# Transfers into the stacks of four attention layers dealt anew over SyncE, ScalarE and GpSimd, in one fused kernel on one core

## The chip, the cores and the metric

One Trainium2 chip, one core. The metric is device time in microseconds of one execution, the median of several runs. Engines: TensorE (PE, with PEld for its weight loads), VectorE (DVE), ScalarE (ACT), GpSimd (POOL), SyncE (SP). Three of them issue DMA transfers here: SP, ACT and POOL; the rows mark these as SPq, ACTq and POOL or POOLq.

## The reference

A picture of 16 x 16 places with 192 channels, batch 1, goes through four residual layers, each with a group norm (32 groups) ahead. All have 12 heads of 16 dimensions and 256 places.

```
x = x + L0(gn(x))   # attention, scores + rel_h (by row) + rel_w (by column)
x = x + L1(gn(x))   # layer norm, attention with rotated q and k and a bias by "same row",
                    # residual, layer norm, feed-forward 192-768-192 with gelu, residual
x = x + L2(gn(x))   # 7x7 neighbourhood attention plus 16 register keys and values
x = x + L3(gn(x))   # like L0, with other weights

qr = q.reshape(B * nh, H, W, hd)                    # the bias of L0 and L3
rel_h = einsum('bhwc,hkc->bhwk', qr, Rh)
rel_w = einsum('bhwc,wkc->bhwk', qr, Rw)
attn = softmax(q * scale @ k.T + rel_h[..., :, None] + rel_w[..., None, :])
```

## The kernel before

Each engine has a program written out by hand, and semaphores order them; no scheduler moves anything. A layer runs so: statistics and norm, projection to queries, keys and values, then scores, exponents, values by head, output projection and residual.

The scores of a head are one matmul over a stack of 128 partitions. QS (queries, two buffers for even and odd layers) and KS (keys) hold for each head four rows for the maxima and the same-place bias and seven blocks of 16 rows (`rows_of(stack, block)` takes one): Q_HIGH, Q_LOW and Q_AGAIN are the high and low parts of queries against the high and low parts of keys (a float32 product made of three float32r ones); ROW_HIGH, COL_HIGH, ROW_LOW, COL_LOW are the terms of the relative bias (L0, L3), of the same-row bias (L1) or of the mask (L2). The parts are computed in tiles that lie by other partitions: QH, QL, KH, KL (96 partitions, two halves of six heads; index 0 and 1), QHL (queries of layers 0 and 3, three groups of four heads), ROWH, ROWL, COLH, COLL (bias terms, three groups). A DMA moves each into its rows of the stack, 96, 64 or 32 KB at a time. ACT makes the high parts, DVE the low ones, right after the projections.

Who waits for what: PE computes each head's scores twice. `for_maxima` (L1014) lays a head's scores by query, DVE takes the maximum (L845), `turn_maxima` (L1028) turns it and ACT copies it into the stack (L631); `scores` (L1050) then computes them by key, ACT takes exponents (L639) and `values` (L1075) multiplies. PE waits before head 0 for the semaphores "q stack", "k stack" and "first rows" (all the transfers of head group 0 or half 0); before head 6 for "later heads" and "later keys" (half 1); in layers 0 and 3 before head 4 for "second heads" and "second queries" and before head 8 for "third heads" and "third queries". The order on PE at a layer's start is: maxima of heads 0, 1, 2, warming matmuls (L936), maxima 3, turn 0, maxima 4, turn 1, scores 0, maxima 5, scores 1, maxima 6, turn 2, maxima 7, values of heads 0 and 1, scores 2, maxima 8. Maxima h may start when DVE has done h - 2 heads.

Who issues: SP's `move` (L336) waits for the signal of its source and issues, in program order, so whatever stands behind a waiting transfer waits too. In layers 1 and 2 it moves by half: QH twice, QL (half 0 of layer 2: POOL), KL. In layers 0 and 3 it moves the queries of group 0, the keys of half 0, then `row_terms` of group 0 and 1, KL of half 1, `row_terms` of group 2; in layer 0 then the later weights (L329). POOL moves the queries of groups 1 and 2 (L464, L467), ROWL of group 0 (L473) and all column terms (L450), in layers 1 and 2 the low rows of half 0's keys (L442), and, after layer 0's last scores, twelve small transfers of the register keys (L523) and four of the mask (L526), which layer 2 needs. Between these POOL computes: bias rows of layer 1 (L495), scaling of key weights (L426), in layer 1 the second half of QF and QL (L514, L516). ACT moves the high keys of half 0 of layers 1 and 2 and both high blocks of half 1 of all layers (L591).

## Time and profile before

| | |
|---|---|
| time, median of 3 runs (lowest to highest) | 154.02 us (153.69 to 154.68) |
| the profiled execution: time, span | 154.34 us, 152.4 us |
| PE busy | 138.8 us (91%) |
| DVE, ACT, POOL busy | 94.3, 68.4, 51.3 us (62, 45, 34%) |
| granted clock of PE | 1.0 over the whole span |
| transfers | 13.55 MB, mean 89 GB/s |

The span is what the profile covers; the time has about 1.9 us more around it. All starts in the rows are counted from the span's start. Layer 0's attention heads begin near 17 us, those of layer 1 near 54, of layer 2 near 98, of layer 3 near 131. Busy shares say little here, since PE is kept busy by warming matmuls too; what counts is where PE waits.

### The profile page before, as it was taken

The page shows a single profiled execution, that of the slowest core. Times are in us where ns is not written, and L with a number is a line of the kernel's source. Part 1 is how long each engine was busy: PE and PEld are TensorE (multiplying, and loading weights), DVE is VectorE, ACT ScalarE, POOL GpSimd, SP SyncE. Part 2 cuts the span into 40 slices and gives each one's busy share as a digit, 9 for nine tenths or more (in the row PEclk, how much of TensorE's full clock was granted, in tenths as well). Part 3 has the DMA queues.
Part 4 walks back from the last instruction along what each step waited for, and adds up shares of the span by engine and source line. Part 5 has one row for each costly group of instructions (what it writes and reads, how often), then busy time and mean ns, then how long its engine had stood idle before and what let it go on. Part 6 is the DMA issues. An engine that isn't in the chain of part 4 may idle for free.

```text
span 152.4 us, 2651 instructions
## 1 busy us (share of the span) xinstructions
PE 138.8 (91%) x914; PEld 93.3 (61%) x914; DVE 94.3 (62%) x246; ACT 68.4 (45%) x158; POOL 51.3 (34%) x92
## 2 busy tenths in 40 slices
PE   6789979999989898999899999689999999979992
PEld 2468656545667575655478747567655679656551
DVE  6885678556749997775630074494546665767462
ACT  4665156842222236770155344055752364166820
POOL 7788988730300499900000002600000077300000
PEclk9999999999999999999999999999999999999999
DMA  5728638999300573900000001900000036810001
GB/s 156 198 54 220 163 97 269 275 275 324 83 0 0 155 163 17 205 0 0 4 0 0 0 0 34 264 13 4 0 0 4 0 114 184 189 33 2 0 0 52
DMA packets 12573, 13.55 MB, mean 89 GB/s; under 512 B 4145, under 2 KB 10433, under 8 KB 12561
## 3 DMA queue, kind: packets, MB, share of 16 engines
q1 hardware_dynamic: 7664, 9.34, 21.5%
q0 software_dynamic: 3424, 2.91, 9.4%
q10 hardware_dynamic: 1472, 1.14, 2.7%
q8 instruction: 7, 0.11, 0.3%
q14 instruction: 6, 0.04, 0.1%
HBM read 6.82 MB, written 0.20 MB: 46 GB/s over the span
## 4 chain that ended last, share of the span: by engine, by line
PE 61%; DVE 13%; DMA 11%; ACT 7%; issue 3%; SPq 3%; POOL 0%; DVEq 0%; ACTq 0%
PE PC L1075 14%; PE RING L1050 8%; DMA KS<-KL 7%; PE RING L936 4%; PE PA L1085 4%; PE RING L1276 4%; PE RING L1014 3%; DVE NM L845 3%; DMA HOT<-in_hot 3%; SPq L336 3%; PE PB L1085 3%; PE PB L1014 2%; PE PA L1282 2%; PE PB L1282 2%; PE PC L971 2%
## 5 line engine op out<-in xcount | busy, mean ns | idle before, releaser
L639 ACT ACTIVATE PR<-RING 128x512 f32<-128x512 f32 (+1 forms) x48 | 25.7, 553 | 9.4 <-PE RING L1050 9.1
L1075 PE MATMUL PC<-PR,VX 128*32 128x256 f32 (+1 forms) x192 | 23.6, 369 | 0.0
L936 PE MATMUL RING<-WARM 128*128 128x512 bf16 x78 | 22.3, 400 | 1.3 <-POOL WARM L395 1.3
L845 DVE TENSOR_REDUCE NM<-RING 128x2 fp32r<-128x512 f32 (+1 forms) x32 | 20.2, 653 | 5.1 <-PE RING L1014 5.1
L1050 PE MATMUL RING<-QS,KS 128*128 128x256 f32 (+1 forms) x96 | 20.2, 305 | 0.4 <-ACT QS L631 0.2
L1050 PEld LDWEIGHTS RING<-QS,KS 128*128 128x128 f32 x96 | 13.9, 189 | 7.8 <-issue 5.1
L631 ACT ACTIVATE QS<-PA 4x512 fp32r<-4x512 f32 (+1 forms) x20 | 10.6, 532 | 15.3 <-PE PA L1028 15.3
L1014 PE MATMUL RING<-KS,QS 128*128 128x256 f32 (+1 forms) x64 | 13.2, 297 | 0.9 <-DVE NM L845 0.8
L1075 PEld LDWEIGHTS PC<-PR,VX 128*32 128x32 f32 x192 | 8.6, 109 | 8.2 <-ACT PR L639 1.3
L852 DVE STREAM_TRANSPOSE TURNED_U<-PC 128x256 f32<-128x256 f32 x12 | 5.4, 450 | 12.8 <-PE PC L1075 12.8
L845 DVE TENSOR_REDUCE NM<-PB 128x2 fp32r<-128x512 f32 (+1 forms) x16 | 10.5, 656 | 4.3 <-PE PB L1014 4.2
L464 POOL DMA_DIRECT2D QS<-QHL x8 | 4.1, 516 | 25.0 <-ACT QHL L614 25.0
L936 PEld LDWEIGHTS RING<-WARM 128*128 128x128 bf16 x78 | 7.5, 107 | 7.1 <-issue 1.4
L1014 PE MATMUL PB<-KS,QS 128*128 128x256 f32 (+1 forms) x32 | 7.4, 312 | 4.2 <-DMA KS<-KL 3.7
L1014 PEld LDWEIGHTS RING<-KS,QS 128*128 128x128 f32 x64 | 9.4, 189 | 3.0 <-DVE NM L845 2.6
L439 POOL DMA_DIRECT2D QS<-QL x1 | 0.5, 538 | 29.8 <-DVE QL L795 29.8
L1014 PEld LDWEIGHTS PB<-KS,QS 128*128 128x128 f32 x32 | 5.0, 188 | 7.5 <-DVE NM L845 2.7
L563 ACT ACTIVATE SQUARED<-X 96x256 f32<-96x256 f32 x8 | 3.3, 415 | 11.4 <-DVE X L909 7.9
L426 POOL TENSOR_SCALAR WQKV<-WQKV 96x384 f32<-96x384 f32 x4 | 5.4, 1362 | 8.8 <-DMA WQKV<-in_w 8.6
L1085 PE MATMUL PA<-O,WO 128*96 128x256 f32 x24 | 7.8, 405 | 0.0
L1085 PE MATMUL PB<-O,WO 128*96 128x256 f32 x24 | 7.1, 379 | 0.0
L495 POOL TENSOR_SCALAR QS<-HOT,ABS 128x256 fp32r<-128x256 f32 x12 | 6.7, 554 | 1.2
(186 smaller groups left out, 270.6 us busy)
## 6 DMA issues: line engine op xcount, KB each, us to landing
WQKV<-in_w SPq DMA_DIRECT2D x2, 576.0 KB, 8.4
WO<-in_wo SPq DMA_DIRECT2D x4, 288.0 KB, 8.9
W<-in_ff SPq DMA_DIRECT2D x2, 576.0 KB, 9.6
KS<-KH ACTq DMA_DIRECT2D x10, 96.0 KB, 3.0
WQKV<-in_w SPq DMA_DIRECT2D x2, 432.0 KB, 4.9
QS<-QHL POOLq DMA_DIRECT2D x12, 64.0 KB, 2.7
KS<-KL SPq DMA_DIRECT2D x8, 96.0 KB, 3.1
QS<-QH SPq DMA_DIRECT2D x8, 96.0 KB, 2.5
```

Of the source, the lines that this page charges most:

```text
L426: g.tensor_scalar(w[:, :, first:first + C], w[:, :, first:first + C], QK_SCALE, None, ALU.mult)\
L495: g.tensor_scalar(QS[1][:, h, :], HOT[:, :], ABS[:, 2, h:h + 1], ABS[:, 1, h:h + 1], ALU.mult, ALU.add).then_inc(sem("ab rows"), 1)
L631: A(QS[l % 2][0:GH, heads[0]:heads[-1] + 1, :], turn_bank(t)[0:GH, None, 0:T].to_broadcast([GH, len(heads), T]), ACT.Copy).then_inc(sem("m ...
L639: A(PR[:, h % NPR, 0:n], exponents(l, h)[:, 0:n], ACT.Exp).then_inc(sem("probs"), 1)
L845: V.tensor_reduce(NM[:, TURN_OF[h], :, h % GH], MAXIMA[h % 3][:, 0:2 * n_keys].rearrange("p (q k) -> p q k", q=2), AX.X, ALU.max, negate=T ...
L936: M(bank, WARM[:, 0:P], WARM[:, :], start=True, stop=True)
L1014: ins = M(s[:, q * n_keys:(q + 1) * n_keys], QS[l % 2][:, h, q * P:(q + 1) * P], KS[:, h, keys], start=True, stop=True)
L1050: ins = M(half(s, l, k), KS[:, h, KEY0 + k * P:KEY0 + (k + 1) * P], QS[l % 2][:, h, reach(l, k)], start=True, stop=True)
L1075: ins = M(columns(h)[:, reach(l, k)], VX[:, k, h, :], half(PR[:, h % NPR, :], l, k), start=(k == 0 and l != 2), stop=(k == 1), skip_group_ ...
L1085: ins = M(y_psum(m), WO[l][:, g, m * CC:(m + 1) * CC], in_order(O[g][:, :]) if l in REL_LAYERS else O[g][:, :], start=(g == 0), stop=(g == ...
L1276: ins = M(s[:, i * T:(i + 1) * T], W1[:, k, c * P:(c + 1) * P], XN[:, k, :], start=(k == 0), stop=(k == NC - 1))
L1282: ins = M(y_psum(m), W2[:, c, m * CC:(m + 1) * CC], hidden(c), start=(c == 0), stop=(c == FM - 1), skip_group_check=True)
```

## The change

The same transfers are made, but for others to issue, and in another order.

- Layers 0 and 3: COLL of group 0 goes from POOL to SP (after the first ROWH pair). ROWL of groups 1 and 2 goes from SP to POOL, behind that group's column terms. ROWH of group 2 goes from SP to ACT, behind the second half's keys. SP's later weights wait for "later heads" and the new "third rows".
- Layer 1: QL goes from SP to POOL, half 0 in place of the low keys, half 1 right after POOL has made it. The low keys of half 0 go from POOL to ACT. The register keys and the mask wait for the first four scores of layer 1 instead of the last of layer 0.
- Layer 2: on SP and on ACT, the moves of half 1 wait for "v psum", the end of the value matmuls (L989).

```diff
@@ SyncE, layers 1 and 2 @@
+                        if i and l == 2:
+                            sync.wait_ge(*upto("v psum", 2, 1))
                         for block in (Q_HIGH, Q_AGAIN):
                             move("qh", rows_of(queries, block)[:, heads], QH[:, i, :], "later heads" if i else "q stack", i + 1)
-                        if i or l == 1:
-                            move("ql", rows_of(queries, Q_LOW)[:, heads], QL[:, i, :], "later heads" if i else "q stack", i + 1)
+                        if i and l == 2:
+                            move("ql", rows_of(queries, Q_LOW)[:, heads], QL[:, i, :], "later heads", i + 1)
@@ SyncE, layers 0 and 3 @@
-                row_terms(0)
-                row_terms(1)
+                high_rows(0)
+                move_group("rel l", COL_LOW, COLL, 0, 4)
+                high_rows(1)
                 move("kl", rows_of(KS, Q_AGAIN, KEY0, REG1)[:, HPC:NH], KL[:, 1, :], "later heads", NC)
-                row_terms(2)
                 if l == 0:
 
-                    sync.wait_ge(*upto("third heads", 0, 4 * 16))
+                    sync.wait_ge(*upto("later heads", 0, 16))
+                    sync.wait_ge(*upto("third rows", 0, 2 * 16))
                     load(later_loads)
@@ GpSimd @@
+            def move_low_rows(l, g, done):
+
+                for r in range(2):
+                    places = slice(r * P, (r + 1) * P)
+                    first = 0 if r else GH
+                    pool.dma_start(rows_of(QS[l % 2], ROW_LOW)[:, g * GH:(g + 1) * GH, places].bitcast(F32),
+                                   ROWL[first:first + 64, g, places].bitcast(F32)).then_inc(sem(done), 16)
...
-                for name, block, src in (("rel h", COL_HIGH, COLH), ("rel l", COL_LOW, COLL)):
+                for name, block, src in (("rel h", COL_HIGH, COLH), ("rel l", COL_LOW, COLL))[:2 if g else 1]:
...
                     for group, done in enumerate(("first rows", "second queries", "third queries")):
+                        if group == 0:
+                            move_low_rows(l, 0, done)
                         move_column_terms(l, group, done)
+                        if group:
+                            move_low_rows(l, group, done)
...
-                    pool.wait_ge(*upto("scores", 0, NH))
+                    pool.wait_ge(*upto("ql", 1, 2))
+                    pool.dma_start(rows_of(QS[1], Q_LOW)[:, HPC:NH].bitcast(F32), QL[:, 1, :].bitcast(F32))\
+                        .then_inc(sem("later queries"), 16)
+
+                    pool.wait_ge(*upto("scores", 1, GH))
@@ ScalarE @@
                 act.wait_ge(*upto("kh", l, i + 1))
+                if i and l == 2:
+                    act.wait_ge(*upto("v psum", 2, 1))
                 heads = slice(i * HPC, (i + 1) * HPC)
-                for block in (Q_HIGH, Q_LOW) if i else (Q_HIGH,):
+                for block in (Q_HIGH, Q_LOW) if i or l == 1 else (Q_HIGH,):
...
                     move_keys(l, 1)
+                    for r in range(2):
+                        places = slice(r * P, (r + 1) * P)
+                        first = 0 if r else GH
+                        act.dma_start(rows_of(QS[l % 2], ROW_HIGH)[:, 2 * GH:NH, places].bitcast(F32),
+                                      ROWH[first:first + 64, 2, places].bitcast(F32)).then_inc(sem("third rows"), 16)
@@ TensorE, before maxima h @@
                 if h == HPC:
+                    if l == 1:
+                        pe.wait_ge(sem("later queries"), 16)
                     pe.wait_ge(*upto("later heads", l, signals["later heads"][l]))
...
-                    pe.wait_ge(*upto(f"{which} heads", l, 4 * 16))
-                    pe.wait_ge(*upto(f"{which} queries", l, 5 * 16))
+                    pe.wait_ge(*upto("second heads" if h == GH else "third rows", l, 2 * 16))
+                    pe.wait_ge(*upto("second queries" if h == GH else "third queries", l, 7 * 16))
```

The order of issues, as it stands in the two programs. GpSimd in layer 0, from ROWL of group 0 to the first instruction that is not a transfer, before (layer 3 has the same):

```order
25 L473 DMA QS<-ROWL 16x4x128 [waits rel_l]
26 L473 DMA QS<-ROWL 16x4x128
27 L450 DMA QS<-COLH 16x4x256 [waits rel_h]
28 L450 DMA QS<-COLL 16x4x256 [waits rel_l]
29 L450 DMA QS<-COLH 16x4x256 [waits rel_h]
30 L450 DMA QS<-COLL 16x4x256 [waits rel_l]
31 L450 DMA QS<-COLH 16x4x256 [waits rel_h]
32 L450 DMA QS<-COLL 16x4x256 [waits rel_l]
33 L411 MEMSET VR 128x384
```

and in the changed kernel (L452 is ROWL, L460 the column terms):

```order
25 L452 DMA QS<-ROWL 16x4x128 [waits rel_l]
26 L452 DMA QS<-ROWL 16x4x128
27 L460 DMA QS<-COLH 16x4x256 [waits rel_h] x2
28 L460 DMA QS<-COLL 16x4x256 [waits rel_l]
29 L452 DMA QS<-ROWL 16x4x128 x2
30 L460 DMA QS<-COLH 16x4x256 [waits rel_h]
31 L460 DMA QS<-COLL 16x4x256 [waits rel_l]
32 L452 DMA QS<-ROWL 16x4x128 x2
33 L413 MEMSET VR 128x384
```

Eight issues have become eleven; the ROWL pair of group 1 stands before the column terms of group 2.

SyncE in layer 0, from the first half's keys on, as a difference:

```order
 L336 DMA KS<-KH 16x6x256 [waits kh]
 L336 DMA KS<-KL 16x6x256 [waits kl]
-L336 DMA QS<-ROWH 16x4x128 [waits rel_h] x4
-L336 DMA QS<-ROWL 16x4x128 [waits rel_l] x2
+L336 DMA QS<-ROWH 16x4x128 [waits rel_h] x2
+L336 DMA QS<-COLL 16x4x256 [waits rel_l]
+L336 DMA QS<-ROWH 16x4x128 [waits rel_h] x2
 L336 DMA KS<-KL 16x6x256 [waits kl]
-L336 DMA QS<-ROWH 16x4x128 [waits rel_h] x2
-L336 DMA QS<-ROWL 16x4x128 [waits rel_l] x2
```

The second KS<-KL, head 6's, is now fifth behind the first instead of sixth, and nothing of this layer's stack follows it.

SyncE in layers 1 and 2 in the changed kernel:

```order
32 L336 DMA QS<-QH 16x6x256 [waits qh,ab_rows]
33 L336 DMA QS<-QH 16x6x256 [waits qh]
34 L336 DMA KS<-KL 16x6x256 [waits kl]
35 L336 DMA QS<-QH 16x6x256 [waits qh] x2
36 L336 DMA KS<-KL 16x6x256 [waits kl]
37 L336 DMA QS<-QH 16x6x256 [waits qh] x2
38 L336 DMA KS<-KL 16x6x256 [waits kl]
39 L336 DMA QS<-QH 16x6x256 [waits qh,v_psum]
40 L336 DMA QS<-QH 16x6x256 [waits qh]
41 L336 DMA QS<-QL 16x6x256 [waits ql]
42 L336 DMA KS<-KL 16x6x256 [waits kl]
```

Rows 32 to 36 are layer 1, where QS<-QL stood before each KS<-KL; 37 to 42 are layer 2, where the wait for v_psum in row 39 is new.

## Rows read from the trace of the kernel before

**Rows 1.** The page: shares of the chain that ended last, by engine (SPq is SyncE issuing)

```profile
PE 61%; DVE 13%; DMA 11%; ACT 7%; issue 3%; SPq 3%; POOL 0%; DVEq 0%; ACTq 0%
```

**Rows 2.** The chain in order of time: start us, us, what

```profile
16.80 5.02 DMA KS<-KL
21.91 0.48 PE PB L1014 x2
...
36.14 0.50 DVE X L909 x2
...
54.79 2.80 DMA KS<-KL
...
94.68 3.40 DMA KS<-KL
98.17 0.44 PE PB L1014 x2
```

**Rows 3.** Timelines of layer 3: start us, us, engine line op out<-in xcount [idle before <-releaser]

```profile
129.93 0.51 POOL L450 DMA_DIRECT2D QS<-COLH  x1
131.11 0.69 DVE L845 TENSOR_REDUCE NM<-PB 128x2 fp32r<-128x512 f32 x1 [0.51 <-PE PB L1014]
...
132.47 0.50 PE L1014 MATMUL RING<-KS,QS 128*128 128x256 f32 x2
...
133.98 0.48 PE L1014 MATMUL PB<-KS,QS 128*128 128x256 f32 x2
...
136.63 0.47 PE L1014 MATMUL RING<-KS,QS 128*128 128x256 f32 x2 [0.77 <-DVE NM L845]
```

**Rows 4.** Landings, layer 3, in flight at 129.95 and 133.55: transfer, queue, KB, us to landing

```profile
QS<-COLH POOLq DMA_DIRECT2D x1, 64.0 KB, 3.2
...
QS<-ROWL SPq DMA_DIRECT2D x1, 32.0 KB, 3.2
```

**Rows 5.** Timelines of layer 0, the issues around the second half's keys

```profile
15.51 1.24 SPq L336 DMA_DIRECT2D QS<-ROWL  x2
15.79 1.31 ACTq L591 DMA_DIRECT2D KS<-KH  x2
15.79 0.48 DVE L795 SCALAR_TENSOR_TENSOR KL<-PC,VECS,KH 96x256 fp32r<-96x256 f32 x1 [0.32 <-ACT KH L584]
...
16.54 0.51 POOL L450 DMA_DIRECT2D QS<-COLH  x1
...
17.82 0.70 DVE L845 TENSOR_REDUCE NM<-PB 128x2 fp32r<-128x512 f32 x1 [0.61 <-PE PB L1014]
```

**Rows 6.** Landings of layer 0: issued at 13.8, at 16.4, at 16.54 and at 17.04

```profile
QS<-ROWL POOLq DMA_DIRECT2D x1, 32.0 KB, 2.5
...
KS<-KH ACTq DMA_DIRECT2D x1, 96.0 KB, 4.9
...
QS<-COLH POOLq DMA_DIRECT2D x1, 64.0 KB, 3.3
...
QS<-COLL POOLq DMA_DIRECT2D x1, 64.0 KB, 4.6
```

**Rows 7.** Timelines of layer 1, DVE and POOL before the heads begin

```profile
53.21 0.74 DVE L789 TENSOR_TENSOR KL<-KF,KH 96x256 fp32r<-96x256 f32 x1
...
53.61 2.04 POOL L523 DMA_DIRECT2D KS<-KRH  x4
...
54.02 0.69 DVE L845 TENSOR_REDUCE NM<-PB 128x2 fp32r<-128x512 f32 x1
```

**Rows 8.** Timelines of layer 2, and the landing of the transfer issued at 97.38

```profile
94.90 1.46 PE L989 MATMUL RING<-WQKV,XN 96*128 96x192 f32 x8
...
97.38 0.68 SPq L336 DMA_DIRECT2D KS<-KL  x1
...
101.30 0.39 PE L1014 MATMUL PB<-KS,QS 128*128 128x192 f32 x2
...
KS<-KL SPq DMA_DIRECT2D x1, 96.0 KB, 2.6
```

More of the change, by code:

```diff
@@ L353, in move_group @@
                     move(signal, rows_of(queries, block)[:, g * GH:(g + 1) * GH], src[:, g, :],
-                         ("q stack", "second heads", "third heads")[g], count)
+                         "q stack", count)
                 def high_queries(g):
@@ L369, in _, with high_rows @@
                 move("kl", rows_of(KS, Q_AGAIN, KEY0, REG1)[:, 0:HPC], KL[:, 0, :], "k stack", 1)
-                def row_terms(g):
-                    for name, block, src in (("rel h", ROW_HIGH, ROWH), ("rel l", ROW_LOW, ROWL))[:2 if g else 1]:
-                        for r in range(2):
-                            places = slice(r * P, (r + 1) * P)
-                            first = 0 if r else GH
-                            move(name, rows_of(queries, block)[:, g * GH:(g + 1) * GH, places], src[first:first + 64, g, places],
-                                 ("q stack", "second heads", "third heads")[g], 2)
-                row_terms(0)
-                row_terms(1)
+                def high_rows(g):
+                    for r in range(2):
+                        places = slice(r * P, (r + 1) * P)
+                        first = 0 if r else GH
+                        move("rel h", rows_of(queries, ROW_HIGH)[:, g * GH:(g + 1) * GH, places], ROWH[first:first + 64, g, places],
+                             ("q stack", "second heads")[g], 2)
+                high_rows(0)
+                move_group("rel l", COL_LOW, COLL, 0, 4)
+                high_rows(1)
                 move("kl", rows_of(KS, Q_AGAIN, KEY0, REG1)[:, HPC:NH], KL[:, 1, :], "later heads", NC)
-                row_terms(2)
                 if l == 0:
-                    sync.wait_ge(*upto("third heads", 0, 4 * 16))
+                    sync.wait_ge(*upto("later heads", 0, 16))
+                    sync.wait_ge(*upto("third rows", 0, 2 * 16))
                     load(later_loads)
@@ L469, in _ @@
                     pool.wait_ge(*upto("rel l", l, 2))
-                    for r in range(2):
-                        places = slice(r * P, (r + 1) * P)
-                        first = 0 if r else GH
-                        pool.dma_start(rows_of(QS[l % 2], ROW_LOW)[:, 0:GH, places].bitcast(F32),
-                                       ROWL[first:first + 64, 0, places].bitcast(F32)).then_inc(sem("first rows"), 16)
                     for group, done in enumerate(("first rows", "second queries", "third queries")):
+                        if group == 0:
+                            move_low_rows(l, 0, done)
                         move_column_terms(l, group, done)
+                        if group:
+                            move_low_rows(l, group, done)
                 if l == 2:
@@ L624, in queries_keys @@
                     move_keys(l, 1)
+                    for r in range(2):
+                        places = slice(r * P, (r + 1) * P)
+                        first = 0 if r else GH
+                        act.dma_start(rows_of(QS[l % 2], ROW_HIGH)[:, 2 * GH:NH, places].bitcast(F32),
+                                      ROWH[first:first + 64, 2, places].bitcast(F32)).then_inc(sem("third rows"), 16)
             def maxima(l, c):
@@ L1004, in for_maxima @@
                 if h in (GH, 2 * GH) and l in REL_LAYERS:
-                    which = "second" if h == GH else "third"
-                    pe.wait_ge(*upto(f"{which} heads", l, 4 * 16))
-                    pe.wait_ge(*upto(f"{which} queries", l, 5 * 16))
+                    pe.wait_ge(*upto("second heads" if h == GH else "third rows", l, 2 * 16))
+                    pe.wait_ge(*upto("second queries" if h == GH else "third queries", l, 7 * 16))
                 for q in range(2):
```

22 lines of the change are left out of this document (11 added, 11 removed).

## The prediction, made blind

> **What bounds it now.** I read the chain of waits first. TensorE (PE) carries 61% of it and a DMA 11%, with another 3% of SyncE issue [rows 1]. PE is the bound almost everywhere, so only the places where it stands still can be won. The chain in order of time says where a DMA releases it [rows 2]. In layer 0 a transfer into KS issued at 16.80 takes 5.02 us, and PE goes on at 21.91. In layer 1 the like transfer ends at 54.79 + 2.80 = 57.6, and PE goes on at about 57.7. In layer 2 one ends at 98.08, PE at 98.17. From head 6 of layer 0 to that layer's residual at 36.14 the chain is nearly all PE: whatever is won before head 6 is won whole.
>
> The heads matter, so I name the matmuls by place. In each layer, L1014 takes heads 0 to 2, then 3, 4, 5, 6 and on. The restart at 21.91 and at 57.7 is head 6, the first of the second half: it waits for KL[:,1] and its fellows. The restart at 98.17 is head 0: layer 2 waits for its first half. Layer 3's stop is another: its head 8 at 136.63 stood idle for 0.77 us [rows 3]. The view names a VectorE (DVE) reduction as releaser, but head 8 needs only the sixth maximum, and six reductions of about 0.6 from 131.11 on are over by 134.8 [rows 3]; a SyncE transfer of ROWL issued at about 133.3 and landing 3.2 us later, at 136.5 [rows 4], is the true one (third heads).
>
> **The change, part by part.** All sums are in microseconds of the profiled execution (span 152.4, its own time 154.34, the median of the runs 154.02); I subtract the sum from the median.
>
> *Layers 0 and 3, the queues.* Number of transfers and bytes stay. An issue costs 0.62 on SyncE (two in 1.24), 0.65 on ScalarE (two in 1.31), 0.51 on GpSimd [rows 5]. SyncE loses six ROWL/ROWH issues to others and takes one COLL. Between the first ROWH pair and KL[:,1] it had four issues (two ROWH, two ROWL), now three. One issue less is 16.80 - 0.62 = 16.2, but DVE makes KL[:,1] from 15.79 for 0.48 [rows 5], so it goes at 16.3 to 16.4. With the same 5.0 to land it is there at 21.4. Its companion KH[:,1] stays: ScalarE's second issue, at about 16.45, landing 4.9 later [rows 6], also 21.3 to 21.4. Both ends: nothing (the landing stretches), and 1.1, if both land by 20.7, where PE's own pace would put head 6: in layer 3 it stands 2.87 after the first reduction (131.11 to 133.98) [rows 3], in layer 0 that reduction begins at 17.82 [rows 5], so 20.7. **Layer 0: 0.5 won.** Head 0's last transfer, COLL, goes one GpSimd issue earlier, from SyncE. In layer 0 that is worth nothing, since transfers set head 6; in layer 3 it is worth between 0 and 0.5, and I take 0, because ROWL sets head 4 there, as follows.
>
> *Head 4 in layers 0 and 3* is where the change costs. It now waits for two ROWL issues of group 1 that stand behind COLH and COLL on GpSimd. Counting 0.51 each, with COLL of group 0 gone, the second ROWL of group 1 is the fifth issue counted from COLH of group 0, and before COLH of group 2 was the fifth; so it goes at that one's time, 16.54 in layer 0 [rows 5] and 129.93 in layer 3 [rows 3]. That COLH, of 64 KB, landed 3.3 and 3.2 later [rows 4, 6]; GpSimd's own ROWL of 32 KB, issued earlier, 2.5 [rows 6]. Between the two I take 2.9. Then layer 0's head 4 starts at 16.54 + 2.9 + 0.15 = 19.6; head 6 follows 1.51 later (132.47 to 133.98 [rows 3]), at 21.1, still before the 21.4 above: hidden. In layer 3 head 4 is at 133.0 instead of 132.47. Head 8 follows head 4 by 136.63 - 0.77 - 132.47 = 3.39, so at 136.4. Group 2's rows are no longer the last: GpSimd issues four more after 129.93, the last at about 132.0, with 3.2 to land by 135.2, where SyncE's landed at 136.5. **Layer 3: 0.2 to 0.3 won, I take 0.3**; the ends are 0 or a loss of 0.1 (3.3 to land) and 0.7 (2.5 to land).
>
> Queued behind these on GpSimd are layer 1's bias rows, three issues or 1.5 later; they are needed by layer 1's heads, which start after 50, so the cover is over 15. ScalarE's two ROWH issues end at about 18.4; its next work is the copy of head 0's maxima, whose reduction begins only at 17.82 and takes 0.70 [rows 5]: covered by a few tenths. SyncE's weights go earlier. All of it I cost at nothing.
>
> *Layer 1.* SyncE had eight issues, now six; QL[:,0] and QL[:,1] go from GpSimd, the low keys of the first half from ScalarE. KL[:,1] is ready when DVE ends at 53.95 [rows 7]; the issue moves from 54.79 to about 54.1. It landed in 2.80 beside GpSimd's twelve register-key transfers, from 53.61 at 0.51 each [rows 7]; these now wait for layer 1's fourth score, near 59.5. So it lands by 56.9, perhaps by 56.5. But then DVE's pace holds: the reduction of head 0 starts at 54.02 because DVE was on KL until 53.95 [rows 7], so the earlier head 0 of the changed kernel gains no more than 0.07, and head 6 comes no sooner than 53.95 + 2.87 = 56.8. **Layer 1: 57.7 to 56.9, 0.8 won**; ends 0.3 (landing 3.3, as in layer 2) and 0.85. The register keys, twelve issues of 0.51 and four of masks, end near 68 and are needed by head 0 of layer 2 (98.17): nothing, with a cover of 30.
>
> *Layer 2.* The second half's six transfers are held until the value matmuls are done: 94.90 + 1.46 = 96.4 [rows 8]. Head 0 waited for KL[:,0], 3.40 from 94.68 [rows 2]; without company from 95.4 on I take the 2.6 that the last transfer of this layer took alone [rows 8]: 97.3, so head 0 at 97.4 to 97.5. The price comes at head 6. SyncE's four issues of 0.61 now start at 96.4, KL[:,1] goes at 98.25 instead of 97.38 [rows 8] and lands at 100.85. Head 6 stood at 101.30, 3.13 after head 0; it could stand at 100.6, and will at 100.9. **Layer 2: 0.4 won**; ends 0.7 (lands at 100.6) and a loss of 0.4 (3.4 to land, 101.7).
>
> **Sum:** 0.5 + 0.8 + 0.4 + 0.3 = 2.0; 154.0 - 2.0 = **152.0 us**.
>
> **The rivals.**
>
> *Same engines, same landing.* The queues share one set of DMA engines, and what lands last depends on the whole load, not on who issued it. For it: KH of 96 KB, COLL of 64 KB and KL, issued at 16.45, 17.04 and 16.80 on three queues, landed within 0.5 of one another (21.3 to 21.8) [rows 2, 6]. Against: layer 1's and 2's gains need only a shorter line. Layer 0 gives 0, layer 3 gives 0: 154.0 - 1.2 = 152.8.
> The Trainium skill states it (Trainium Kernel Development and Optimization, Key Constraints): transfers from SP, ACT and POOL run on the same 16 engines, and issuing from several saves only issue time. By that rule the trace agrees in layer 0, where three queues ended together.
>
> *ROWL late for head 4.* If GpSimd's fourth transfer takes 3.6 in both layers, head 6 of layer 0 is at 16.54 + 3.6 + 0.15 + 1.51 = 21.8 (0.1 won), head 8 of layer 3 at 137.1 (0.5 lost): 1.2 - 0.4 = 0.8 won, 153.2.
>
> *The same, far enough to be slower.* With L the landing, layer 0 loses L - 3.71 and layer 3 L - 3.12. Together with the 1.2 of the other layers the kernel is slower from L = 4.0 on, and by over 1% from L = 4.8. The longest of GpSimd's in these rows is 4.6, for COLL at 17.04 [rows 6], behind one issue more. At 5.0 the time is 156.0.
> The Trainium skill has a mechanism for such a delay (SBUF — State Buffer, the box on "DVE blocks DMA"): some VectorE copies lock GpSimd out while it writes descriptors. No row here shows it.
>
> *Layer 2's second half late.* KL[:,1] takes 3.4 as the first did: 0.4 lost instead of won, 152.8.
>
> *Everything comes free.* Layer 0 1.1, layer 1 0.85, layer 2 0.7, layer 3 0.77: 3.4, 150.6.
>
> **Chances.** Forecast 0.50; same landing 0.15; ROWL late 0.12; slower 0.04; layer 2 late 0.07; everything 0.12. What this measurement can tell from no change is about 1%, 1.54 us, so the border is 152.48. Below it lie the forecast but for its upper edge (0.46), all of the last case and a sixth of the three middle ones (0.06): 0.64. Slower by 1%: 0.04. The rest, 0.32, is within 1%. The range is 151.0 to 153.3: it leaves out the slower case, most of the last and little of ROWL late.
>
> **What would show it.** Head 6 of layer 0 near 21.4 and of layer 1 near 56.9; head 0 of layer 2 near 97.4 and its head 6 near 100.4 to 100.9 as PE allows; head 4 of layer 3 about 0.5 later after head 0 than before, yet no idle before head 8. All measured from the layer's own start, since the layers move up. Wrong would be: PE idle before head 4 of over 1 us in layer 0 or 3; a wait at head 6 of layer 2 longer than the one gained at head 0; landings of 5 us still there at head 6 of layer 0 with KL issued at 16.4 or before.

## The result and the profile after

| | before | after |
|---|---|---|
| time, median (lowest to highest) | 153.86 us (153.17 to 154.68, 4 runs) | 157.17 us (156.21 to 158.25, 4 runs) |
| ratio after/before | | 1.0215, 95% interval 1.012 to 1.0309 |
| profiled execution: time, span | 154.34, 152.4 us | 158.25, 156.4 us |

The changed kernel is slower by 2% (1.2 to 3.1), not faster by 1.3%. A ratio here and below leaves out the executions that took over 1.5% longer than the fastest of their kernel, while a median counts them all. The page of after: the row of PE in part 1, three rows of part 2, the chain's shares.

```profile
PE 141.5 (90%) x906; PEld 96.0 (61%) x914; DVE 94.7 (61%) x246; ACT 68.6 (44%) x158; POOL 55.5 (35%) x99
...
PE   6999928999998969999989999978999999889992
...
PEclk9999996999999999999999999999999999999999
DMA  5716562999800055037300000550000017630001
...
PE 69%; DVE 11%; DMA 7%; ACT 4%; issue 3%; POOL 2%; SPq 1%; ACTq 0%; DVEq 0%; POOLq 0%
```

Two things stand out in slices 6 and 7 of 40 (19.6 to 27.4 us): PE's row has a hole (2), and the clock row, 9 all over before, has a 6. PE's waits and the chain around the hole say what they are (waits: us in total, times, longest; chain: start us, us, what; the maxima of a head are L1034 now):

```profile
PE RING L1034 <- DMA QS<-ROWL: 3.4, 1, 3.4
PE RING L955 <- POOL WARM L397: 1.3, 1, 1.3
PE PB L1034 <- DMA KS<-KH: 1.2, 1, 1.2
PE RING L1034 <- DVE NM L864: 1.1, 1, 1.1
```
```profile
7.87 0.85 PE PC L1173 x2
...
18.31 0.49 POOL QS L452
18.80 5.07 DMA QS<-ROWL
24.01 0.47 PE RING L1034 x2
...
55.13 3.33 DMA KS<-KH
58.55 0.48 PE PB L1034 x2
```

At 24.01 head 4 of layer 0 starts, after 3.41 of idling, on the second ROWL transfer of group 1, which the change has put on GpSimd: issued at 18.80, it took 5.07 to land. What follows is in the windows of after (busy us of PE, PEld, DVE, ACT, POOL, then granted clock, DMA share, GB/s):

```profile
20.00:22.00 2.00, 0.60 (x5) 0.42 (x4) 1.72 (x3) 0.37 (x1) 1.91 (x5) 1.00 0.86 224
22.00:24.00 2.00, 0.00 (x0) 0.02 (x1) 0.00 (x0) 0.00 (x0) 1.54 (x7) 1.00 0.29 69
24.00:26.00 2.00, 1.99 (x11) 1.99 (x12) 1.01 (x2) 0.97 (x2) 1.70 (x4) 0.59 0.00 1
26.00:28.00 2.00, 2.00 (x11) 1.09 (x9) 1.76 (x3) 1.19 (x2) 1.70 (x4) 0.55 0.85 251
28.00:30.00 2.00, 2.00 (x17) 1.43 (x16) 1.21 (x2) 1.45 (x3) 1.70 (x4) 1.00 1.06 344
```

After the idle stretch the granted clock is 0.59 and 0.55, so mostly at the lower of its two levels (1.2 instead of 2.4 GHz), and back at 1.00 from 28 on. Before, it was 1.0 throughout.
The Trainium skill (TensorE: Matmul & The Clock Gate, Part 1) says that an idle TensorE is taken back to 1.2 GHz; the trace agrees, with 3.41 us of idling and 0.59 behind it.

To see where the 4.0 us of span went, I cut both traces at the same matmuls and issues. The timeline of before at head 9 of layers 0 and 3 and head 0 of layer 3, then that of GpSimd at the first COLH of layers 0 and 3:

```profile
24.26 0.40 PE L1014 MATMUL PB<-KS,QS 128*128 128x256 f32 x2
130.60 0.47 PE L1014 MATMUL PB<-KS,QS 128*128 128x256 f32 x2 [0.22 <-DMA QS<-COLL]
137.34 0.39 PE L1014 MATMUL PB<-KS,QS 128*128 128x256 f32 x2
```
```profile
14.53 0.51 POOL L450 DMA_DIRECT2D QS<-COLH  x1 [0.24 <-ACT COLH L622]
...
127.92 0.51 POOL L450 DMA_DIRECT2D QS<-COLH  x1 [0.24 <-ACT COLH L622]
```

And of after: the first two COLH of layer 0 and the first of layer 3; then heads 0 and 9 of layer 0, head 6 of layer 1, head 0 of layer 2, heads 0, 4 and 9 of layer 3:

```profile
16.51 0.51 POOL L460 DMA_DIRECT2D QS<-COLH  x1 [0.24 <-ACT COLH L636]
17.29 0.51 POOL L460 DMA_DIRECT2D QS<-COLH  x1 [0.27 <-ACT COLH L636]
...
132.25 0.51 POOL L460 DMA_DIRECT2D QS<-COLH  x1 [0.24 <-ACT COLH L636]
```
```profile
18.69 0.50 PE L1034 MATMUL PB<-KS,QS 128*128 128x256 f32 x2
29.00 0.40 PE L1034 MATMUL PB<-KS,QS 128*128 128x256 f32 x2
62.25 0.47 PE L1034 MATMUL PB<-KS,QS 128*128 128x256 f32 x2 [0.20 <-DVE NM L864]
102.51 0.44 PE L1034 MATMUL PB<-KS,QS 128*128 128x192 f32 x2 [0.92 <-DMA KS<-KL]
134.46 0.51 PE L1034 MATMUL PB<-KS,QS 128*128 128x256 f32 x2
137.49 0.47 PE L1034 MATMUL RING<-KS,QS 128*128 128x256 f32 x2 [1.12 <-DVE NM L864]
141.33 0.40 PE L1034 MATMUL PB<-KS,QS 128*128 128x256 f32 x2
```

| stretch | before | after | difference | forecast |
|---|---|---|---|---|
| start to the first COLH of layer 0 | 14.53 | 16.51 | +1.98 | 0 |
| first COLH to head 9, layer 0 | 9.73 | 12.49 | +2.76 | -0.5 |
| to head 6 of layer 1 (57.69 before) | 33.43 | 33.25 | -0.18 | -0.8 |
| to head 0 of layer 2 (98.17 before) | 40.48 | 40.26 | -0.22 | -0.4 |
| to head 0 of layer 3 | 32.43 | 31.95 | -0.48 | (0) |
| to head 9 of layer 3 | 6.74 | 6.87 | +0.13 | (-0.3) |
| to the end of the span | 15.1 | 15.1 | 0 | 0 |

The differences add up to 3.99 of 4.0. The first row is ahead of everything the change touches: in this execution the first projections ran at 0.85 a pair, and the start differs from one execution to the next (0.42 instead of 1.98 in e1_again, whose first COLH of layer 0 goes at 14.95; in k_l1 below, where nothing of layer 0 is changed, it went at 17.58). The loss that belongs to the change is the second row.

### The profile page after: what moved, and what is told of

It reads as the page before. It is cut to its first block, busy times and chain, and to the rows that moved or that the text cites. A ratio compares the mean times of both kernels' runs of the same rounds, so it can differ in the third digit from the quotient of the medians.

```text
span 156.4 us, 2647 instructions
## 1 busy us (share of the span) xinstructions
PE 141.5 (90%) x906; PEld 96.0 (61%) x914; DVE 94.7 (61%) x246; ACT 68.6 (44%) x158; POOL 55.5 (35%) x99
## 4 chain that ended last, share of the span: by engine, by line
PE 69%; DVE 11%; DMA 7%; ACT 4%; issue 3%; POOL 2%; SPq 1%; ACTq 0%; DVEq 0%; POOLq 0%
PE PC L1095 14%; PE RING L1070 10%; PE RING L955 8%; PE RING L1034 4%; PE PA L1105 4%; DVE NM L864 4%; PE RING L1296 3%; DMA QS<-ROWL 3%; PE PB L1105 3%; PE PB L1034 2%; DMA KS<-KH 2%; DMA KS<-KL 2%; PE PA L1173 2%; PE PA L1302 2%; PE PB L1302 2%
## 5 line engine op out<-in xcount | busy, mean ns | idle before, releaser
L955 PE MATMUL RING<-WARM 128*128 128x512 bf16 x71 | 21.6, 418 | 1.6 <-POOL WARM L397 1.3
L1070 PEld LDWEIGHTS RING<-QS,KS 128*128 128x128 f32 x96 | 14.4, 194 | 7.8 <-issue 5.3
L1034 PE MATMUL RING<-KS,QS 128*128 128x256 f32 (+1 forms) x64 | 13.7, 307 | 4.5 <-DMA QS<-ROWL 3.4
L1034 PEld LDWEIGHTS RING<-KS,QS 128*128 128x128 f32 x64 | 10.0, 198 | 6.4 <-issue 3.8
L440 POOL DMA_DIRECT2D QS<-QL x2 | 1.1, 550 | 31.7 <-DVE QL L814 22.9
L1034 PE MATMUL PB<-KS,QS 128*128 128x256 f32 (+1 forms) x32 | 7.5, 318 | 2.3 <-DMA KS<-KH 1.2
L428 POOL TENSOR_SCALAR WQKV<-WQKV 96x384 f32<-96x384 f32 x4 | 5.9, 1477 | 9.8 <-DMA WQKV<-in_w 9.6
L1034 PEld LDWEIGHTS PB<-KS,QS 128*128 128x128 f32 x32 | 5.2, 197 | 4.8 <-issue 3.1
```

Source lines behind the costliest of these rows:

```text
L428: g.tensor_scalar(w[:, :, first:first + C], w[:, :, first:first + C], QK_SCALE, None, ALU.mult)\
L955: M(bank, WARM[:, 0:P], WARM[:, :], start=True, stop=True)
L1034: ins = M(s[:, q * n_keys:(q + 1) * n_keys], QS[l % 2][:, h, q * P:(q + 1) * P], KS[:, h, keys], start=True, stop=True)
L1070: ins = M(half(s, l, k), KS[:, h, KEY0 + k * P:KEY0 + (k + 1) * P], QS[l % 2][:, h, reach(l, k)], start=True, stop=True)
```

## The experiments

My first theory (A) was the queue: ROWL of group 1 stands too far back, PE waits at head 4 and then loses clock. Against it stood, among others, chance at the start (B), one DMA engine behind the others whatever the order (D), ScalarE's queue as such (F), and full engines (E): what group 2 and the second half put beside group 1's last transfers makes these land late, whatever queue has them. Lines of code differ by a few between kernels; "head 0 to head 9" is the distance between the starts of their maxima matmuls in the profiled execution. The least seen is 5.71 to 5.74, in both layers of h_l1only and h_e3hold, in layer 3 of j_late and in layer 0 of k_l2; I call it PE's own pace. Before needed 6.95 in layer 0 and 6.74 in layer 3, since its second half's keys and group 2's rows came late.

### Which part loses

**e1_again**: the changed kernel once more.

> The changed kernel once more, every part of the change in. Theory A (queue): the time lost is PE's wait before head 4 of layer 0 (3.41 us in the first profile), for ROWL issued at 18.8 by GpSimd and landed 5.1 later, with PE's granted clock at 0.59 and 0.55 in the 4 us behind it. Then it is there again: a wait of 2.5 to 4 us, 156 to 158 us, ratio 1.015 to 1.03. Theory B (chance): in the first profile PE ran its matmuls at half the rate until about 10.3 us against 4.5 us in the kernel before, 1.4 us later at head 0. If that is what the change costs, the wait is small here and the time moves by under 1 us when PE's rate rises early. Both can hold: then the profiles differ by 1.4 us with the rise.

Median 157.0 (154.05 to 157.89, 4 runs) beside 154.59 of before; head 4 of layer 0 waits 2.86 for ROWL, and the granted clock behind it is 0.62. The loss repeats.

**e2_layers03**: the edits of layers 0 and 3 alone. **e3_layers12**: those of layers 1 and 2 alone.

```diff
@@ e2_layers03, against the changed kernel: layers 1 and 2 as before @@
-                        if i and l == 2:
-                            sync.wait_ge(*upto("v psum", 2, 1))
...
-                    pool.wait_ge(*upto("scores", 1, GH))
+                    pool.wait_ge(*upto("scores", 0, NH))
@@ e3_layers12: the other way round, the queues of layers 0 and 3 as before @@
```

> Only the parts of the change in layers 0 and 3 (COLL to SyncE, ROWL of groups 1 and 2 to GpSimd, ROWH of group 2 to ScalarE); layers 1 and 2 as before. Theory A: all of the loss and a little more, 156.5 to 158 us, since layers 1 and 2 do not lose by the change. Theory C (the loss is in the middle): no slower than before, 153 to 154.5 us.

> Only the parts in layers 1 and 2 (QL to GpSimd, low keys to ScalarE, register keys later, layer 2's second half held); layers 0 and 3 as before. Theory A: 0.3 to 0.8 us faster than before, 153.1 to 153.6 us, by the 0.8 that layer 1 gained from its start to its end in the first profile and the 0.1 to 0.3 that layer 2 lost or gained. Theory C: over 1 us slower.

e2: median 156.68, ratio 1.0142 (1.0031 to 1.0254), head 4 of layer 0 waits 3.18. e3: 152.71, ratio 0.9923 (0.9877 to 0.9969), head 4 waits 0.19, head 6 of layer 0 comes at 21.02, the clock is 1.0 throughout. The whole loss is in the queues of layers 0 and 3; the parts for layers 1 and 2 gain.

### Is it GpSimd, or the transfer's turn?

Four kernels share the question. **e4_rowl_sync** is the changed kernel with ROWL of groups 1 and 2 back on SyncE. **e6_coll** and **e7_rowl** have, beside the parts for layers 1 and 2, one edit of layers 0 and 3 each: only COLL of group 0 on SyncE, or only ROWL of groups 1 and 2 on GpSimd. **e5_rowh2** has only ROWH of group 2 on ScalarE.

```diff
@@ e4_rowl_sync, against the changed kernel @@
                 high_rows(1)
+                low_rows(1)
                 move("kl", rows_of(KS, Q_AGAIN, KEY0, REG1)[:, HPC:NH], KL[:, 1, :], "later heads", NC)
+                low_rows(2)
...
-                        if group:
-                            move_low_rows(l, group, done)
```

> The changed kernel with ROWL of groups 1 and 2 back on SyncE; all other parts in. Theory A: head 4 waits for SyncE's ROWL as before, under 0.5 us, and PE's clock stays at 1.0: 152.5 to 153.6 us. Theory B: as the changed kernel when PE's rate rises late (156 and over). If the landing is slow whoever issues it (theory D, one DMA engine behind the others in layer 0 whatever the order), a wait of 2 us or more stays somewhere before head 6 of layer 0: 155 to 157 us.

> Layers 1 and 2 as changed, and of layers 0 and 3 COLL of group 0 from SyncE alone: SyncE waits for it and issues ROWL of group 1 and the second half's keys 0.6 to 1.2 later (17.4 instead of 16.3 for the last ROWL). Theory E: that pushes the last ROWL behind ScalarE's two transfers of 96 KB, it lands 4 to 5 later, head 4 waits 2 to 3.3 us in both layers, with PE's clock falling behind it: 155.5 to 158 us. Theory F: no wait, 152.5 to 153.2 us.

> Layers 1 and 2 as changed, and of layers 0 and 3 ROWL of groups 1 and 2 from GpSimd alone, behind the column terms: COLL of group 0 is on GpSimd too, so the last ROWL of group 1 goes at 17.3 to 17.8. Theory E: head 4 waits over 2.5 us in layer 0, 155 to 158 us. Under theory F: below 1 us of waits.

> Layers 1 and 2 as changed (the faster kernel of the last runs, 152.7 us), and of layers 0 and 3 one part alone: ROWH of group 2 from ScalarE. Theory E (full engines: whatever of group 2 and half 1 is issued beside group 1's last transfers makes these land late, in one lump near 21.5 to 22 us in layer 0): two more transfers at 17.2 and 17.9 on a third queue, ROWL of group 1 still issued by 16.2 and landing within 3.5; no wait at head 4 over 0.5 us, 152.4 to 153.2 us. Theory F (it is ScalarE's queue as such that holds the others up): a wait of over 2 us at head 4.

| | ratio (95%) | last ROWL of group 1, layer 0 | head 4 waits |
|---|---|---|---|
| e4_rowl_sync | 1.027 (1.0202 to 1.0338) | SyncE, 17.4, 4.9 to land | 3.2 |
| e6_coll | 1.0326 (1.0231 to 1.0421) | SyncE, 19.1, 4.4 | 2.9 |
| e7_rowl | 1.0169 (1.0108 to 1.0229) | GpSimd, 19.1, 4.6 | 2.7 |
| e5_rowh2 | 0.9991 (0.9938 to 1.0044) | SyncE | none |

Landings in e4_rowl_sync in flight at 17.4, then PE's waits of the same kernel:

```profile
QS<-COLL POOLq DMA_DIRECT2D x1, 64.0 KB, 4.8
...
QS<-ROWL SPq DMA_DIRECT2D x1, 32.0 KB, 4.9
```
```profile
PE RING L1064 <- issue: 6.5, 2, 3.3
```

It is not GpSimd. In layer 0 the last ROWL of group 1, of 32 KB, lands in 4.4 to 5.1 from either queue once it goes behind ScalarE's second transfer of keys (in layer 3 of after it took 2.8 at the same place); in e4_rowl_sync a COLL on GpSimd, issued at 17.1, is just as late. e6_coll shows how little it takes: one COLL on SyncE, the edit that I had costed at nothing in layer 0, has SyncE's last ROWL go 2.57 behind GpSimd's first COLH instead of the 1.56 of e3_layers12, so 1.0 later, and PE waits 2.9.
The Trainium skill (Trainium Kernel Development and Optimization, Key Constraints) has all three queues on the same 16 engines; the trace agrees, as 4.9 on SyncE and 4.8 on GpSimd in e4_rowl_sync show.
It is not ScalarE's queue either (F): in e6_coll and e7_rowl that queue is as before and head 4 waits all the same, and in e5_rowh2, where it alone is longer, head 4 does not wait. There the second KL takes 5.7 instead of the 3.7 of e3_layers12, and head 6 stands for 1.42. Whether the added ROWH does that isn't shown: the same KL took 5.0 in before and 5.9 in j_l2only below, both without it, and the ratios can't tell the two kernels apart.

What such a landing is made of can be read from the semaphores in the kept traces. Every transfer raises its semaphore sixteen times, and the landing in these rows is the time when the count is full. In layer 0 of after the second KL, alone on its semaphore, had 15 of its 16 raises by 21.94 and the last at 23.48. The two ROWL of group 1 had 30 of their 32 by 22.16, the others at 23.15 and 23.88, and PE went at 24.01. In e4_rowl_sync, with ROWL on SyncE, it was 31 of 32 by 20.80 and the last at 22.30. In layer 3 of after, where nothing was late, 31 had come by 137.29 and the last at 137.35. So the transfer is not slow as a whole: one part in sixteen comes about 1.5 to 2 us behind the rest, on whatever queue. This is what theory D describes, one engine behind the others; that it is one engine, and which, the traces don't tell, and no run was made to test it.

### Make the load lighter, or the transfer earlier

**e8_hold**: the changed kernel with group 2's transfers on GpSimd and ScalarE held until head 1's maxima matmuls are done. **h_first**: group 1's and 2's ROWL ahead of their column terms, in the same queue. **h_firsthold**: both.

```diff
@@ e8_hold, GpSimd; the same wait on ScalarE ahead of ROWH of group 2 @@
                     for group, done in enumerate(("first rows", "second queries", "third queries")):
+                        if group == 2:
+                            pool.wait_ge(*upto("max psum", l, 2))
@@ h_first, GpSimd @@
-                        if group == 0:
-                            move_low_rows(l, 0, done)
+                        move_low_rows(l, group, done)
                         move_column_terms(l, group, done)
-                        if group:
-                            move_low_rows(l, group, done)
```

> The changed kernel, but GpSimd and ScalarE hold group 2's transfers until the scores of head 1 for the maxima are done (about 18.0 in layer 0). Theory E: with fewer transfers beside it ROWL of group 1, issued at 17.3, lands 0.5 to 2 earlier than in the changed kernel (it shares the engines only with the second half's keys, 288 KB), so head 4 waits 1 to 2.5 us instead of 2.9 to 3.4, 153.5 to 156 us. If the wait stays at 2.9 or more, group 2 is not what makes it late, and it is either the second half's keys or one engine behind the others.

> The changed kernel with the two ROWL transfers of groups 1 and 2 (layers 0 and 3) issued on GpSimd ahead of their group's COLH and COLL instead of behind them. The number of issues before the last transfer of group 1 stays; only which one is last changes. (E) Full engines: what goes last lands last. ROWL is in time, but now COLL of group 1 lands 4.5 to 5 after its issue, head 4 of layer 0 still waits 2.5 to 3 us, for COLH or COLL, and the time is the changed kernel's, 156 to 158. (S) It is ROWL itself, small pieces to 64 partitions, that is slow: issued two issues (1.0 us) earlier it lands 1 us earlier at least, COLL takes about 3, head 4 waits under 1.5 us, the granted clock does not fall, and the time is 153 to 155. I give E two in three.

> As h_first, and in addition the transfers of group 2 held until the maxima of head 1 are begun, as in e8_hold. (E) The last transfer of group 1 lands in about 3, as ROWL did in e8_hold: head 4 waits about 0.8, time 154 to 156. (S) ROWL earlier and COLL fast: no wait at head 4, 152.5 to 154. In both, layer 0's second half of keys still sets head 6 (near 22).

Heads 4 and 6 of layer 0 in e8_hold, and the landings in flight at 17.1; then the same two heads of h_first and its landing at 16.75; then head 4 of h_firsthold and its window behind it:

```profile
20.18 0.47 PE L1069 MATMUL RING<-KS,QS 128*128 128x256 f32 x2 [0.80 <-DMA QS<-ROWL]
22.47 0.47 PE L1069 MATMUL PB<-KS,QS 128*128 128x256 f32 x2 [0.68 <-DMA KS<-KH]
...
KS<-KH ACTq DMA_DIRECT2D x1, 96.0 KB, 5.6
...
QS<-ROWL POOLq DMA_DIRECT2D x1, 32.0 KB, 3.0
```
```profile
19.86 0.47 PE L1069 MATMUL RING<-KS,QS 128*128 128x256 f32 x2 [0.77 <-DMA QS<-COLL]
22.31 0.47 PE L1069 MATMUL PB<-KS,QS 128*128 128x256 f32 x2 [0.83 <-DMA KS<-KH]
...
QS<-COLL POOLq DMA_DIRECT2D x1, 64.0 KB, 3.0
```
```profile
20.57 0.47 PE L1069 MATMUL RING<-KS,QS 128*128 128x256 f32 x2 [1.55 <-DMA QS<-COLL]
...
22.00:24.00 2.00, 2.00 (x12) 1.21 (x10) 1.70 (x3) 1.26 (x3) 1.60 (x5) 0.52 0.46 126
```

Ratios 1.0064 (1.0012 to 1.0117), 1.0062 (0.9997 to 1.0127) and 1.0049 (0.9994 to 1.0104). In the profiled execution with group 2 held, the same ROWL from the same queue takes 3.0 instead of 5.1. That the load beside it made it late is not shown by this: KH, issued 0.34 ahead of that ROWL, still took 5.6, with one late raise again (31 of the 32 of its pair by 20.30, the last at 22.34), so the late part is still there and has missed ROWL. Nor did holding help at the same place when ROWL went first: COLL took 3.0 in h_first and 3.6 in h_firsthold. In h_first COLL is last, 64 KB, issued at 16.74 and there in 3.0, so in this execution being last was not enough to be late; whether ROWL's shape matters is not shown, since e4_rowl_sync had a COLL that took 4.8.

How much of the loss is gone is less than these ratios say. The medians of all ten executions are 155.91, 156.48 and 155.43, beside 153.71, 154.08 and 154.08 of before: 2.2, 2.4 and 1.35 lost, where the changed kernel lost 3.3 and, in e1_again, 2.4. The mean granted clock was 0.989 or lower in six, eight and seven of the ten, and in seven of the changed kernel's eight. The profiles of e8_hold and h_first caught executions at clock 1.00 and are not typical of these kernels; h_first's median is even the 156 to 158 that its expectation gave theory E. That either edit helps in most executions is not shown.

They also say something of how much idling the clock bears. In the profiled executions 0.77 and 0.83 (h_first), 0.80 and 0.68 (e8_hold) and 0.94 before head 6 (before) left it at 1.00; 1.55 (h_firsthold) brought 0.52. The length of one stretch does not decide it alone, for in layer 3 of e6_coll 1.63 left it at 1.00:

```profile
137.52 0.47 PE L1069 MATMUL RING<-KS,QS 128*128 128x256 f32 x2 [1.63 <-DMA QS<-ROWL]
...
138.00:140.00 2.00, 1.92 (x16) 1.50 (x16) 1.92 (x3) 1.70 (x4) 0.00 (x0) 1.00 0.21 56
```

Over all executions: of 106 of before beside the experiments 99 had a mean granted clock of 0.995 or more; of the changed kernel's 8, one (154.05 us, its fastest); of h_firsthold's 10, three (153.4 to 153.8 us) against 155.0 to 157.3 for the other seven.

### Wait or clock

**j_fill**: the changed kernel with warming matmuls in the idle stretch ahead of head 4, and nothing else. **j_late**: e3_layers12, where nothing of layers 0 and 3 is moved, with a later condition for head 4 of layer 0.

```diff
@@ j_fill, TensorE, before maxima h @@
                 if h in (GH, 2 * GH) and l in REL_LAYERS:
+                    if h == GH:
+                        keep_warm(MAXIMA[1][:, :], {0: 12, 3: 6}[l])
@@ j_late, TensorE: head 4 of layer 0 waits for what head 8 needs too @@
-                    for name in ("second heads", "second queries") if h == GH else ("third heads", "third rows", "third queries"):
+                    for name in (("second heads", "second queries") if h == GH else ()) + \
+                            (("third heads", "third rows", "third queries") if h == 2 * GH or l == 0 else ()):
```

> The changed kernel with matmuls of the WARM tile (128x512, 0.60 for two) put ahead of head 4: twelve in layer 0 and six in layer 3, so that TensorE works while it waits for ROWL. The transfers are not touched. (G) The fall of the granted clock comes from the idle stretch: with it filled the rows from 22 to 28 stay at 1.00, head 4 still comes about 3 late (filler included), and the time is about 2 below the changed kernel's, 154 to 155.5, most executions at a mean clock of 0.99 or more instead of 0.989 and below. (H) The clock falls for another reason at that point, or the filler's own time (3.0 if TensorE takes 0.25 each) costs what it saves: 156 to 158. I give G three in four.

> e3_layers12 (the parts for layers 1 and 2 alone) with one wait more: head 4 of layer 0 waits also for all that head 8 needs, which lands near 22.5; no transfer is moved. So TensorE stands for about 3 us there as in the changed kernel. (G) The idle stretch alone brings the whole loss: head 4 at 22.6, the granted clock near 0.5 for 4 us behind it, mean clock 0.989 in the executions, time 152.7 + 2 (head 4 to head 9 of the changed kernel less what head 6 waited anyway) + 2 (clock) = 156 to 157. (H) The clock needs more than the idling: 154.5, clock 1.0.

j_fill: the filler, heads 4 of layers 0 and 3, and the window behind the first. j_late: head 4 of layer 0 and two windows.

```profile
18.88 2.76 PE L991 MATMUL RING<-WARM 128*128 128x512 bf16 x12
22.09 0.48 PE L1073 MATMUL RING<-KS,QS 128*128 128x256 f32 x2 [0.45 <-DMA QS<-ROWL]
...
136.14 0.47 PE L1073 MATMUL RING<-KS,QS 128*128 128x256 f32 x2 [1.41 <-DMA QS<-ROWL]
...
22.00:24.00 2.00, 1.88 (x15) 1.71 (x16) 1.34 (x3) 1.12 (x3) 1.69 (x4) 1.00 0.01 3
```
```profile
23.37 0.76 PE L1073 MATMUL RING<-KS,QS 128*128 128x256 f32 x2 [3.81 <-DMA QS<-ROWL]
...
22.00:24.00 2.00, 0.63 (x3) 0.62 (x4) 0.00 (x0) 0.00 (x0) 1.70 (x4) 0.50 0.06 18
24.00:26.00 2.00, 2.00 (x12) 1.96 (x11) 1.35 (x2) 1.20 (x3) 1.70 (x4) 0.50 0.88 270
```

j_late: median 157.7, ratio 1.0278 (1.0227 to 1.0329), above the 156 to 157 expected. An idle stretch of 3.81 with no transfer moved does all that the change does, clock included. j_fill: the clock stays at 1.00 there, and at 0.997 or more in all four executions, so idling is what lowers it. But the time is 156.62, ratio 1.0204 (1.016 to 1.0247), the changed kernel's own; I expected 154 to 155.5. In layer 0 the clock's share can be read: from head 4 to head 9 j_fill takes 25.95 - 22.09 = 3.86, e1_again 4.98, after 29.00 - 24.01 = 4.99, so 1.1 us of the loss in these profiles is clock. The times don't bear it out: j_fill's executions, all at full clock, are no faster than the changed kernel's. This profile lost it again in layer 3, where the last ROWL took 4.7 to land (2.8 in after) and head 9 came 8.58 behind head 0 instead of 6.87. Whether the filler has a part in that is open.

### The terms for layers 1 and 2, and a better kernel

**h_l1only**, **j_l2only**: before with layer 1's edits, or layer 2's wait, alone. **k_both**, **k_l1**, **k_l2**: e3_layers12 and these two again, on one chip. **h_e3hold**: e3_layers12 with the hold of group 2's column terms of e8_hold.

> The kernel before with layer 1's part of the change alone (its low keys from ScalarE, low queries from GpSimd, register keys held until its fourth score); layers 0, 2 and 3 as before. By my sum layer 1 is worth 0.8 of the 1.2 of e3_layers12: ratio 0.995, head 6 of layer 1 standing 0.2 or less for a reduction, about 3.7 us behind head 0, and layer 2's head 0 waiting 1.5 us or so for a KS transfer as before. If layer 2's hold is worth nothing (its gain at head 0 given back at head 6), the ratio is that of e3_layers12, 0.992. If it is layer 2 that gives it, 0.999.

> The kernel before with layer 2's hold alone (its second half's transfers held until the value matmuls are done). From head 6 of layer 1 to head 0 of layer 2 the kernel before takes 40.48, e3_layers12 40.14: 0.3 gained and kept, ratio 0.998. If layer 1's register keys, which stay early here, and this hold do nothing together: 1.000. Together with h_l1only at 1.000 a ratio of 0.992 would say that layer 2 gives all of e3_layers12.

> e3_layers12 once more (the parts for layers 1 and 2 alone), to be compared on one chip with k_l1 and k_l2. If its 0.8% was of the parts, the ratio is 0.990 to 0.995 again. If h_l1only and j_l2only at 1.000 tell the truth and the parts only add up, it is 0.998 to 1.000, and the first 0.992 was chance in the kernel before on that chip. From the traces (from head 9 of layer 0 to head 6 of layer 2, PE's own starts, the changed parts save 0.2 + 0.3) I expect 0.996.

> Layer 1's part alone once more, beside k_both. From the traces it is worth 0.0 to 0.3 us (head 9 of layer 0 to head 6 of layer 1: 33.43 before, 33.43 and 33.15 with the part): ratio 0.998 to 1.000.

> Layer 2's part alone once more, beside k_both. From the traces it is worth 0.3 us (head 6 of layer 1 to head 0 of layer 2: 40.48 before, 40.1 with it): ratio 0.998.

> e3_layers12 (the parts for layers 1 and 2 alone) with GpSimd's COLH and COLL of group 2 in layers 0 and 3 held until the maxima of head 1 are begun. (E) Full engines: with these two, of 64 KB each, out of the way, KL and KH of the second half land sooner: head 6 of layer 0 in 4 instead of 5 us after their issue, worth 0 to 0.4; time 152.3 to 152.7, ratio 0.990 to 0.992. If the lump at 21.5 comes from the second half's keys themselves nothing changes: 152.7. If group 2 becomes late for head 8, 0.5 to 1 more: 153.5.

| | ratio (95%), median |
|---|---|
| h_l1only; k_l1 | 0.9999 (0.9952 to 1.0046), 153.69; 0.9951 (0.9917 to 0.9985), 152.91 |
| j_l2only; k_l2 | 0.9999 (0.9964 to 1.0033), 153.86; 0.9988 (0.9944 to 1.0032), 153.77 |
| e3_layers12; k_both | 0.9923 (0.9877 to 0.9969), 152.71; 0.996 (0.9919 to 1.0), 153.05 |
| h_e3hold | 0.99 (0.9842 to 0.9958), 152.78 |

On one chip both parts give 0.996, layer 1's alone 0.995, layer 2's alone 0.999: some 0.6 us in all (0 to 1.2 by the interval), which is the expected 0.996, and the 0.992 of e3_layers12 was probably in part luck in layers 0 and 3. Its trace points to that: from head 9 of layer 0 to head 6 of layer 1 it takes 33.43, as before, from there to head 0 of layer 2 40.14 instead of 40.48, and head 0 to head 9 took 5.97 in layer 0 and 5.98 in layer 3, though nothing there was changed. h_e3hold has the lowest ratio, with both those stretches at 5.74 in its profile (issued at 17.2, the second KL lands in 3.3, where it took 5.0 before). Its lead over e3_layers12 lies within the intervals, and its median is no lower (152.78 beside 152.71). j_l2only, whose queues in layer 0 are those of before, warns that these too can lose: in its profiled execution (157.81) the second KL took 5.9, with 15 of 16 raises by 20.80 and the last at 22.98, head 6 stood for 1.94, and the clock behind it was at 0.68 and 0.50. The change makes frequent what before shows in 7 of 106 executions.

## Why the prediction was wrong

**Head 4 in layers 0 and 3: the step that failed.** I let the last ROWL of group 1 go at the time of before's COLH of group 2 [rows 5], 2.01 behind the first COLH, and took 2.9 to land. It went 18.80 - 16.51 = 2.29 behind it: with COLL of group 0 off the queue the second COLH has to wait 0.27 for ScalarE to make it. That is 0.28 of the miss. The landing is the rest: 5.07 for 2.9, from rows of transfers that went ahead of the crowd, or (COLH, 3.3) landed early within it. Before's own COLL at 17.04, 4.6 [rows 6], was the nearest row in place and load, and I used it only for a rival. Head 4 came 24.01 - 16.51 = 7.50 behind the first COLH instead of 5.07, which is these 2.4, and no longer hidden behind head 6's keys. Then 1.1 us of lower clock came on top, which no term or rival had: the price of a wait on PE was taken as its length. In layer 3 the same transfer took 2.8, and the term came out as forecast: from the first COLH to head 9 9.42 before and 9.08 after, 0.34 won for 0.3.

**Layers 0 and 3, the queues.** Wrong in what it rests on: that the second half's keys would set head 6 near 21.4, 0.5 earlier, as KL landed in 5.0. KL did land 0.3 earlier, 6.97 behind the first COLH instead of 7.29. But its companion KH landed 7.57 behind it instead of 6.89, so head 6 would have gained nothing even without the wait of head 4, which came on top. That COLL of group 0 on SyncE brings nothing was wrong too: from the first COLH to head 0 before takes 2.78, after 2.18, and layer 3's head 0 is 0.48 earlier behind layer 2's. I had given it 0 to 0.5 there.

**Layer 1.** Right in mechanism, too large in size. Head 6 does follow DVE's pace ([0.20 <-DVE NM]) and comes 3.70 behind head 0 instead of 4.18. But I took head 0's own time as fixed. It now waits for the low keys from ScalarE, 55.13 + 3.33 (shown above), and comes 0.30 later behind head 9 of layer 0 than before. 0.8 was 0.18 net, and from 0.15 lost to 0.4 won in the other traces with this part; k_l1's ratio allows 0.2 to 1.3.

**Layer 2.** Right, within its bounds: KL lands in 3.17 instead of the 2.6 I took, head 0 gains 0.22 (0.34 in e3_layers12), and head 6 stays 3.13 behind head 0, so nothing is given back. 0.4 was forecast.

**The rivals.** *The same, far enough to be slower* named the place and the transfer. With its own L of 5.07 it gives 1.36 lost in layer 0, against 2.76 measured from the first COLH on: it lacked the clock and the later issue (its 3.12 for layer 3 should be 3.16 by its own rows, which changes nothing). Its chance of 0.04 rested on L in both layers being far out; one layer was enough. *Same engines, same landing* held for the landings of the second half's keys (still 5.0 and 5.6), but I had let it stop at "nothing won".

What stays open is why the same transfer, at the same place in the order, lands in 3 or in 5: what differs is whether one of its sixteen parts comes 1.5 to 2 us behind the others, and why it does is not known. The last ROWL of group 1 took 5.1 in layer 0 and 2.8 in layer 3 of one execution, and 4.9 and 4.7 in j_fill; the second KL of layer 0 took 5.0 before, 3.7 in e3_layers12, 4.2 in h_l1only, 5.3 in j_late and 5.9 in j_l2only, with the same queues.

## What to carry to other kernels

When several queues feed one set of transfer engines, an issue that goes later, on whatever queue, can take on a much longer landing: price it with the longest landing seen at that place and load, not with that of a transfer which went ahead of it. Holding back what is not needed yet looked good in single profiles here and is not shown by the times. Look at several executions before a profile is called typical: a part that is late in one of them may not be in the next. A wait of TensorE has a price above its length once it lasts long enough for the granted clock to fall, so look at the clock row before calling a wait of 2 or 3 us covered by slack. And a gain at one head is real only measured from an anchor that the change does not touch.
